# Attention's elementwise work on pairs of token tiles, and the query projection in two halves

## The reference

```python
h = layernorm(x) * (1 + ca) + sa
x = x + ga * attn(h)
h = layernorm(x) * (1 + cb) + sb
x = x + gb * ffn(h)

# attn: no softmax; a projection, elementwise work, a group norm and a transposition
Q = relu(rope_rotate(X @ W_Q))       # rotation of pairs in the first 64 of 512 channels
H = tanh(Q + hh_b)
out = group_norm(H, 32 groups of 16 channels) * weight + bias
out = swapaxes(out, -2, -1).reshape(B, T, C)

# ffn: weights are a table of 16 values looked up by an index
h = silu(x @ lut[gate_idx].T) * (x @ lut[up_idx].T)    # 1376 hidden channels
y = h @ lut[down_idx].T
```

## Time and profile before

| | before |
|---|---|
| median of 3 executions | 1061.77 us |
| the profiled execution | 1063.87 us |
| its span, first to last instruction | 1061.6 us |
| TensorE matmuls busy | 960.3 us (90%), 4480 |
| VectorE busy | 603.0 us (57%), 1384 instructions |
| ScalarE busy | 410.0 us (39%), 621 |
| GpSimd busy | 185.2 us (17%), 156 |
| loads of 1 MB of x by L241, median to landing | 6.2 us |

### The profile page before, as it was taken

The page is one execution under the profiler, slowest core; times in us unless marked ns, Lnnn a source line. Parts: engine busy times, 40 slices in busy tenths (PEclk is TensorE's granted clock), DMA queues, the critical chain, the costliest instruction groups (busy, mean ns, idle before and its releaser), DMA issues.

```text
span 1061.6 us, 13109 instructions
## 1 busy us (share of the span) xinstructions
PE 960.3 (90%) x4480; PEld 464.8 (44%) x4480; DVE 603.0 (57%) x1384; ACT 410.0 (39%) x621; POOL 185.2 (17%) x156
## 2 busy tenths in 40 slices
PE   5869669977888988999899999999999999999998
PEld 5534326433333433444444444444444444444443
DVE  5599995997589874334887876322222432222312
ACT  2365854566554633224543532332222421222200
POOL 3111202036456540112202200110000101000000
PEclk9989887988899999999999999999999999999999
DMA  8667363531001021234235114222000112000011
GB/s 291 214 178 218 68 185 64 178 100 40 20 20 30 20 80 50 80 110 119 40 119 158 32 48 159 80 70 89 0 0 0 55 44 102 0 0 0 1 40 40
DMA packets 33740, 83.40 MB, mean 79 GB/s; under 512 B 2977, under 2 KB 2977, under 8 KB 30625
## 3 DMA queue, kind: packets, MB, share of 16 engines
q1 hardware_dynamic: 32544, 74.47, 21.4%
q0 software_dynamic: 1152, 8.39, 4.3%
HBM read 63.98 MB, written 18.87 MB: 78 GB/s over the span
## 4 chain that ended last, share of the span: by engine, by line
PE 68%; DVE 17%; issue 6%; ACT 5%; DMA 1%; SPq 1%; POOL 1%; DVEq 0%; ACTq 0%; POOLq 0%
PE ps L1163 27%; PE ps L1197 22%; PE ps L1130 7%; PE ps L1152 4%; DVE hid L834 3%; PE ps L1118 2%; DVE R L856 2%; PE ps L1175 2%; PE ps L1210 2%; DMA w_all<-wmod_dram 1%; DVE hd L865 1%; ACT R L571 1%; DVE st L750 1%; ACT w_all L562 1%; PE ps L1142 1%
## 5 line engine op out<-in xcount | busy, mean ns | idle before, releaser
L1163 PE MATMUL ps<-h,w_all 128*128 128x512 f16 x1920 | 424.7, 383 | 18.8 <-DVE hd L865 16.3
L1163 PEld LDWEIGHTS ps<-h,w_all 128*128 (+1 forms) x1920 | 188.5, 99 | 252.3 <-issue 19.5
L1197 PE MATMUL ps<-w_all,hid 128*128 128x512 f16 x1056 | 231.1, 381 | 4.7 <-DVE w_all L1047 4.7
L1197 PEld LDWEIGHTS ps<-w_all,hid 128*128 128x128 f16 x1056 | 103.6, 98 | 129.5 <-DVE w_all L1047 5.2
L865 DVE SCALAR_TENSOR_TENSOR hd<-ps,col,sg 128x512 f32<-128x512 f32 x80 | 59.9, 748 | 149.5 <-ACT sg L532 149.5
L532 ACT ACTIVATE sg<-ps,col 128x512 f32<-128x512 f32 x80 | 54.6, 682 | 181.8 <-PE ps L1163 181.1
L890 DVE SCALAR_TENSOR_TENSOR hd<-ps,col,gbB 128x512 f32<-128x512 f32 x32 | 24.0, 751 | 148.4 <-PE ps L1197 148.1
L1152 PE MATMUL ps<-hid,w_all 128*128 128x512 f16 x352 | 90.1, 419 | 12.9 <-DVE hid L834 12.9
L547 ACT ACTIVATE hid<-hd 128x512 f16<-128x512 f32 (+1 forms) x88 | 55.0, 628 | 113.0 <-DVE hd L865 99.7
L1130 PE MATMUL ps<-WQ,work 128*128 128x512 f16 x384 | 89.1, 394 | 4.0 <-DVE col L980 3.1
L427 POOL TENSOR_TENSOR h<-h,h 128x512 f16<-128x512 f32 x32 | 37.3, 1186 | 306.5 <-ACT h L517 306.5
(11 more groups left out here) (112 smaller groups left out, 840.6 us busy)
## 6 DMA issues: line engine op xcount, KB each, us to landing
R<-x_dram SPq DMA_DIRECT2D x16, 1024.0 KB, 6.9
xa<-x_dram SPq DMA_DIRECT2D x14, 1024.0 KB, 6.2
hid<-idx_dram SPq DMA_DIRECT2D x44, 256.0 KB, 6.9
R<-bias_dram POOLq DMA_DIRECT2D x8, 1024.0 KB, 8.4
out_dram<-R SPq DMA_DIRECT2D x32, 256.0 KB, 2.2
x_dram<-R SPq DMA_DIRECT2D x7, 1024.0 KB, 5.0
w_all<-wmod_dram SPq DMA_DIRECT2D x6, 1024.0 KB, 15.2
h<-idx_dram SPq DMA_DIRECT2D x11, 256.0 KB, 2.6
```

Of the source, the lines that this page charges most:

```text
L1163: ins = nc.tensor.matmul(bank(GU[2 * s + t]), W[wp][:, bass.ds(at, P)], h2[hp][:, s, k], start=(k == 0 and i == 0), stop=(k == K - 1 and i ...
L1197: ins = nc.tensor.matmul(bank(QY[par]), hid[hp][:, bass.ds(at, P)], W[wp][:, w_at:w_at + BLK], start=(j == 0 and i == 0), stop=(j == J - 1 ...
```

## The change

All of it lies in attention. The matmuls and the values computed are the same.

- `rope_relu`, `tanh`, `center`, `square` and `sum_squares` take two neighbouring token tiles per instruction. A block has two of each where it had four. The products with the tables are split by even and odd channel instead of by tile, so that there are four for a pair, as before; all other instructions halve in number and double in width. A pair waits for both of its tiles.
- `project` makes one pair, and is called twice in a block. Between the calls TensorE does a weight sum (batch 0) or a gate unit (batch 1) that stood behind the projection. The second pair waits until both banks of the first are taken.
- The written order of VectorE and ScalarE around them is another: the statistics of the next block now stand right behind the first rotation; the centring of the first pair comes after them; on ScalarE the normalisation and (batch 0) `summed_out(w, 0)`, or (batch 1) a silu, stand ahead of the second tanh, and the squares of the first pair behind it.

```diff
-            def tanh(n, a):
-                act.wait_ge(pre_tanh, A * n + a + 1)
-                nc.scalar.activation(H[:, a], H[:, a], ACT.Tanh, scale=c_isq).then_inc(tanh_ready, 1)
+            def tanh(n, pair):
+                a = 2 * pair
+                act.wait_ge(pre_tanh, A * n + a + 2)
+                nc.scalar.activation(H[:, a:a + 2], H[:, a:a + 2], ACT.Tanh, scale=c_isq).then_inc(tanh_ready, 2)
...
+            def square(n, pair):
+                a = 2 * pair
+                act.wait_ge(centered, A * n + a + 2)
+                reach(act, sq_summed, A * n + a)
+                nc.scalar.activation(sq[:], H[:, a:a + 2], ACT.Square).then_inc(squared, 2)
...
 # ScalarE, batch 0
                 tanh(q, 0)
                 half_idx(w + 3, 1)
-                tanh(q, 1); square(q, 0); tanh(q, 2); square(q, 1)
                 if not last:
                     norm(q + 1)
-                tanh(q, 3)
                 summed_out(w, 0)
-                square(q, 2); square(q, 3)
+                tanh(q, 1)
+                square(q, 0)
+                square(q, 1)
                 if not last:
                     half_idx(w + 4, 0)
                 summed_out(w + 1, 1)
...
 # ScalarE, batch 1
-                        tanh(n, 0); tanh(n, 1); square(n, 0); tanh(n, 2); square(n, 1)
+                        tanh(n, 0)
                         if not last:
                             norm(m + 1)
-                        tanh(n, 3)
                         attn_unit_silu(q, 0)
-                        square(n, 2)
+                        tanh(n, 1)
+                        square(n, 0)
                         attn_unit_silu(q, 1)
                         for h in range(2):
                             if not last:
                                 affine(...)
                             if h == 0:
-                                square(n, 3)
+                                square(n, 1)
...
+            def rope_relu(n, q, pair):
+                a, half = 2 * pair, ROPE // 2
                 reach(dve, pre_tanh, A * n + a)
+                reach(dve, sq_summed, A * n)
+                dve.wait_ge(q_ready, A * n + a + 2)
+                Q = ps[:, QY[0] * BLK:(QY[0] + 2) * BLK].rearrange("p (a n) -> p a n", a=2)
...
+                for e in range(2):
+                    Qe = Q[:, :, 0:ROPE].rearrange("p a (i e) -> p e a i", e=2)[:, e]
+                    v.tensor_tensor(rot[:, e], Qe, table(cosT), ALU.mult)
+                    ins = v.tensor_tensor(tmp[:, e], Qe, table(sinT), ALU.mult)
+                step(ins)
+                v.tensor_tensor(rot[:, 0], rot[:, 0], tmp[:, 1], ALU.subtract)
+                step(v.tensor_tensor(rot[:, 1], rot[:, 1], tmp[:, 0], ALU.add))
+                over = lambda t: t.unsqueeze(1).broadcast_to((P, 2, t.shape[1]))
+                v.scalar_tensor_tensor(H[:, a:a + 2, ROPE:], Q[:, :, ROPE:], 0.0, over(hhS[:, ROPE:]),
+                                       ALU.max, ALU.add).then_inc(q_taken, 2)
...
 # center, sum_squares: the same instructions on H[:, a:a + 2] and sq[:]
...
 # VectorE, batch 0
                 masks(w + 1, 1)
-                rope_relu(q, q, 0); rope_relu(q, q, 1); center(q, 0); rope_relu(q, q, 2); center(q, 1)
+                rope_relu(q, q, 0)
                 if not last:
                     stats(q + 1)
-                rope_relu(q, q, 3)
-                sum_squares(q, 0); center(q, 2); sum_squares(q, 1); center(q, 3)
+                center(q, 0)
+                rope_relu(q, q, 1)
+                sum_squares(q, 0)
+                center(q, 1)
                 if not last:
                     masks(w + 2, 0)
-                sum_squares(q, 2); sum_squares(q, 3)
+                sum_squares(q, 1)
...
 # VectorE, batch 1
-                        rope_relu(n, q, 0); rope_relu(n, q, 1); center(n, 0); rope_relu(n, q, 2); center(n, 1)
+                        rope_relu(n, q, 0)
                         if not last:
                             stats(m + 1)
-                        rope_relu(n, q, 3)
-                        sum_squares(n, 0); center(n, 2); sum_squares(n, 1); center(n, 3)
+                        center(n, 0)
                         attn_hidden(q, 0)
-                        sum_squares(n, 2); sum_squares(n, 3)
+                        rope_relu(n, q, 1)
+                        sum_squares(n, 0)
+                        center(n, 1)
                         attn_hidden(q, 1)
+                        sum_squares(n, 1)
                         group_scale(n, 1)
...
 # TensorE
+            def project(n, m, y_before, pair):
+                if pair == 0:
+                    pe.wait_ge(lo_ready, K * (m + 1))
+                    reach(pe, o_ready, y_before)
+                reach(pe, q_taken, A * n + 2 * pair)
+                for a in (2 * pair, 2 * pair + 1):
...
-                project(q, q, 0)
+                project(q, q, 0, 0)
                 sum_chunk(w, 0, True)
+                project(q, q, 0, 1)
                 sum_chunk(w + 1, 1)
...
-                        project(n, m, A * S * g)
+                        project(n, m, A * S * g, 0)
                         gate_up(g, 2 + 2 * q, 0)
+                        project(n, m, A * S * g, 1)
                         gate_up(g, 2 + 2 * q, 1)
```

More of the change, by code:

```diff
@@ L769, in rope_relu @@
                 at = (q * A + a) * half
[L770 to L776, removed]
@@ L777, in rope_relu @@
-                v.tensor_tensor(rot2[:, 0], rot2[:, 0], tmp2[:, 1], ALU.subtract)
-                step(v.tensor_tensor(rot2[:, 1], rot2[:, 1], tmp2[:, 0], ALU.add))
-                v.scalar_tensor_tensor(H[:, a, ROPE:], Q[:, ROPE:], 0.0, hhS[:, ROPE:], ALU.max, ALU.add) \
-                 .then_inc(q_taken, 1)
-                v.scalar_tensor_tensor(H[:, a, 0:ROPE], gs2[:, 0:ROPE], 0.0, hhS[:, 0:ROPE],
-                                       ALU.max, ALU.add).then_inc(pre_tanh, 1)
-            def center(n, a):
-                dve.wait_ge(tanh_ready, A * n + a + 1)
-                Hg = H[:, a].rearrange("p (g e) -> p g e", e=GSZ)
-                sums = gs[:, 0, a * GRP:(a + 1) * GRP]
+                table = lambda t: t[:, at:at + 2 * half].rearrange("p (a i) -> p a i", a=2)
@@ new lines, in rope_relu @@
+                rot, tmp = (gs[:, i].rearrange("p (a i e) -> p e a i", a=2, e=2) for i in (2, 3))
+                for e in range(2):
[5 more added lines that the diff above has]
+                step(v.tensor_tensor(rot[:, 1], rot[:, 1], tmp[:, 0], ALU.add))
@@ new lines, in rope_relu, with center @@
+                over = lambda t: t.unsqueeze(1).broadcast_to((P, 2, t.shape[1]))
+                v.scalar_tensor_tensor(H[:, a:a + 2, ROPE:], Q[:, :, ROPE:], 0.0, over(hhS[:, ROPE:]),
+                                       ALU.max, ALU.add).then_inc(q_taken, 2)
+                v.scalar_tensor_tensor(H[:, a:a + 2, 0:ROPE], gs[:, 2].rearrange("p (a n) -> p a n", a=2), 0.0,
+                                       over(hhS[:, 0:ROPE]), ALU.max, ALU.add).then_inc(pre_tanh, 2)
+            def center(n, pair):
+                a = 2 * pair
+                dve.wait_ge(tanh_ready, A * n + a + 2)
+                Hg = H[:, a:a + 2].rearrange("p a (g e) -> p (a g) e", e=GSZ)
+                sums = gs[:, 0, a * GRP:(a + 2) * GRP]
@@ L789, in center @@
                 step(v.tensor_reduce(sums, Hg, axis=AX, op=ALU.add))
-                v.scalar_tensor_tensor(Hg, sums.unsqueeze(2).broadcast_to((P, GRP, GSZ)), -1.0 / GSZ, Hg,
+                v.scalar_tensor_tensor(Hg, sums.unsqueeze(2).broadcast_to((P, 2 * GRP, GSZ)), -1.0 / GSZ, Hg,
                                        ALU.mult, ALU.add) \
-                 .then_inc(centered, 1)
-            def sum_squares(n, a):
-                dve.wait_ge(squared, A * n + a + 1)
-                v.tensor_reduce(gs[:, 1, a * GRP:(a + 1) * GRP], sq[:, a % 2].rearrange("p (g e) -> p g e", e=GSZ),
-                                axis=AX, op=ALU.add).then_inc(sq_summed, 1)
+                 .then_inc(centered, 2)
@@ L799, in group_scale, with sum_squares @@
+            def sum_squares(n, pair):
+                a = 2 * pair
+                dve.wait_ge(squared, A * n + a + 2)
+                v.tensor_reduce(gs[:, 1, a * GRP:(a + 2) * GRP], sq.rearrange("p a (g e) -> p (a g) e", e=GSZ),
+                                axis=AX, op=ALU.add).then_inc(sq_summed, 2)
             def group_scale(n, b, masks_par=None):
```

13 lines of the change are left out of this document (removed).

## The result

The changed kernel takes 1100.99 us (median of 4, 1100.11 to 1101.9) against 1061.92 us of the kernel before (median of 4, one execution more than above, 1061.48 to 1063.47). The ratio is 1.0361, with a 95% interval of 1.0342 to 1.0379: 3.6% slower, where 1090.8 us, 2.7% and at most 1099 us had been forecast. (The ratios are formed from all executions and not from the medians, so they differ a little from the quotient of these.) The profiled execution took 1101.9 us with a span of 1099.6 us, so the span grew by 38.0 us where the prediction's sum was 29.0. Between the medians the miss is 10.2 us, since the execution profiled before lay 2.1 us above the median that the prediction started from, and this one 0.9 above its own. The time lies in the range of the prediction's rival "grouping pays nothing, or the clock falls" (1099 to 1105).

A forecast was written before the change was run, and what follows sets the result against it. The order of VectorE and ScalarE in the attention blocks was taken as the bound; delays of 3*2.85+4.8+6.4+9.3, called 29.0 us, make 1063.87 into 1092.9, less 2.1 for the median: 1090.8 us, range 1079 to 1099.

The forecast's parts named there:

- grouping pays nothing, or the clock falls: Rival, attention blocks: pair forms cost twice the single ones, or TensorE's clock drops after longer gaps; 1099 to 1105 us, chance 0.06.
- The squares behind the second tanh: VectorE idles before the first sum of squares, waiting for ScalarE's square: 3.0 us a block in batch 0, 2.4 in batch 1.
- The wait for a pair: VectorE idles about 2 us ahead of each block's first rotation, until TensorE has projected both tiles.
- T+24.65: Batch 0's last block, T its projection's start: group scaling begins 6.4 us later than before, as no statistics fill the gap.
- Prices of the pair forms: VectorE and ScalarE in attention: fixed part plus cost per element, saving VectorE 1.6 us a block.
- the 13 us reckoned: VectorE's work over all eight attention blocks: 1.6 us a block saved by pair forms, 13 us in all.
- The load of x: Batch 0's first three blocks: statistics wait for the next block's x by 0.8, 1.6 and 2.4 us, 4.8 in all.
- the failed step: Batch 1's blocks, T the projection's start: group scaling 2.1 us later in three blocks, 3.0 in the last, 9.3 in all.
- The TensorE half is no limit: Batch 0's first three blocks: sum and projection matmuls end at R+8.7, R being two tiles projected, ahead of the second rotation.
- the faster rival: Rival, VectorE from first rotation to masks: its own work sets the block's end, so 1.6 us a block comes through; 1048.9, chance 0.04.

The follow-up runs named there:

- the pairs undone: The changed kernel with every paired instruction replaced by two of one tile, same order and same waits for pairs: 1108.79 us, ratio 1.0415.
- The filling: The changed kernel with unused matmuls in TensorE's two idle stretches at each block's end in batch 1: 1096.20 us, ratio 1.0308.
- the mended mixture: The mixture with last blocks on single tiles, x loaded earlier in both batches, batch 1's second squares behind the affine's first half: 1064.39 us, ratio 1.0008.
- the split alone: The kernel before with only the projection in two halves, a weight sum or gate unit between, elementwise work on single tiles: 1089.56 us, ratio 1.0237.
- the mixture: The changed kernel with projection whole, first two tiles' rotation and tanh single, first squares earlier, x earlier in batch 0, batch 1 reordered: 1067.93 us, ratio 1.0055.
- the repairs together: The changed kernel with first squares ahead of the second tanh, x loaded earlier in both batches, unused matmuls filling TensorE in batch 1: 1073.77 us, ratio 1.0102.

## Why the prediction was right in direction and short by 9 us

- **The squares behind the second tanh.** Forecast 3.0 us a block in batch 0, measured 2.69 to 2.83; in batch 1 forecast 2.4, measured 2.29. Taking the wait away gave back 20.2 us, so it is shown, and it is as heavy as priced.
- **The wait for a pair.** Forecast 2 us ahead of the first rotation, measured 2.34 in the second block and 1.85 in the third. In batch 0's last block the group scaling was forecast at T+24.65, 6.4 us later; it came at T+24.82, 6.6 later.
- **Prices of the pair forms.** Rotation pair 2.33 us from its start to the next operation's (562.39 to 564.72), forecast 2.3; sum and centring 107.17 to 109.63, 2.46, forecast 2.4; tanh 1.15 (1.24), square 1.05 (1.14): ScalarE's slope was taken from an operation with another input type and priced a little dear. VectorE saved the 13 us reckoned, when seen from the pairs undone; the 8.3 between before and after are less, in part by the 2.5 of the collision.
- **The load of x.** Forecast waits of 0.8, 1.6 and 2.4 us, measured 0.59, 1.50 and 1.05: the third load landed in 7.5 us and not in 8.8. Taking the waits away gave 2.3 us. The reason that the prediction gives for the long landing, the store ahead of it in the queue, was not tested.
- **Batch 1, the failed step.** "group scaling at T+29.25, before at 559.88 = T+27.16: 2.1 later", and the sum "3\*2.1+3.0 = 9.3". It came 1.1 later still, at T+30.34. In the three blocks group scaling is 3.4, 3.2 and 3.0 us later than before, 9.6 instead of 6.3: 3.3 us, of which the centring's longer duration is 2.5. The step took the duration of an operation from a place where GpSimd was idle. Before, the last centring began at T+22.0 and ended 2.2 us ahead of GpSimd's low parts; on pairs it begins at T+25.6, beside them.
- **The clock, the other half of the failed step.** The prediction looked at the 2.62 us of idle time in the earlier trace rows and said that it was there already. It did not count that the first transposes would idle too. Cost: the second transposes 0.5 to 0.7 us in four blocks, 2.5 us; the last block's projection 6.93 instead of 5.34, 1.6 us; the matmuls behind it 2.0 us. That is 6.1 us, and with 3.3 it makes 9.4 of the 9.6 missed in batch 1. The filling gave back 4.8 between the medians and 6.2 in the profile. The rival that named the clock had the mechanism ("longer gaps could bring that to more blocks, some 1.5 each") and should have been part of the sum, not a rival with a chance of 0.06. That the time lies in its range is partly luck: its other half, pair forms that save nothing, is out by the pairs undone.
- **"The TensorE half is no limit"** held in the changed kernel. My later belief that the split was therefore dispensable did not: undoing it cost 23 us.
- **Grouping as a gain.** The mechanism behind the faster rival, VectorE's work as the limit, held in no run. In the changed kernel 8 of 13 us came through, in the mended mixture none that can be told. The Trainium skill (Perfetto Trace Analysis, Optimizing Scalar/DVE Operations) has both halves of this: larger operations help a saturated engine, and where an engine isn't saturated but makes others idle, smaller ones can end sooner. VectorE, 54% busy, is not saturated here, and the 2.34 us that it waits for a pair's second tile point to the second half; but with the pairs' waits kept, smaller instructions were slower by 7.8 us, and no run took only the waits away.

## What to carry to other kernels

When two tiles share an instruction, write down for each engine what stands between the pair's producer and its consumer in program order, and move the consumer's supplier first: three moved lines were worth half of the loss. An operation that moves in time takes its price from what runs beside it at the new time, and where TensorE gains a second gap, ask what a lower clock behind it would cost. Two edits that come together have to be measured in all four combinations before one is blamed: here the split alone cost 27 us, the pairs with their new order and no split 61, both together 39.

## What the runs showed that I had not expected

- A 128x1024 product on VectorE took 2.20 us instead of 1.23 beside a GpSimd tensor operation, and 1.23 again when that was moved. Beside GpSimd's next two low parts (586.71, 2.42 us) 128x128 ones took 1.13 instead of 0.29 us, in the changed kernel's rows here and in the kernel before as well (561.70 and 562.86):

```profile
586.65 0.29 DVE L736 TENSOR_TENSOR gs<-gs 128x128 f32<-128x128 f32 x1
586.98 1.13 DVE L738 SCALAR_TENSOR_TENSOR gs<-gs 128x128 f32<-128x128 f32 x1
588.15 1.13 DVE L740 SCALAR_TENSOR_TENSOR gs<-gs 128x128 f32<-128x128 f32 x1
```

- 84 matmuls that compute nothing made the kernel 4.8 us faster, by keeping the granted clock up where TensorE had stood idle for 2.15 and 2.74 us.
- A load of 1 MB issued 0.3 to 0.5 us ahead of GpSimd's DMA took 12.3 to 13.4 us to land (four loads, in the changed kernel with the earlier load and in the mixture), against 7.5 to 8.5 at the changed kernel's place and 5.4 where it was issued ahead of the last index table, in the repairs together. Whether GpSimd's DMA is the reason was not tested by itself.
